# Self-attention of a decoder layer: ends reordered, two repeating loads, and the query product as three fp32r products

## The reference, cut to what matters

```python
def _L0_attn_ref(x, Wq, Wk, Wv, Wu, bu):            # x: (16, 224, 512), 16 heads of 32
    xh = x.reshape(b, t, h, c)
    scale = d ** (-0.25)
    q = jnp.einsum('bthc,oc->btho', xh, Wq) * scale
    k = jnp.einsum('bthc,oc->btho', xh, Wk) * scale
    v = jnp.einsum('bthc,oc->btho', xh, Wv)
    scores = jnp.einsum('bihc,bjhc->bhij', q, k)     # causal mask on j > i
    attn = jax.nn.softmax(scores, axis=-1)
    y = jnp.einsum('bhij,bjhc->bihc', attn, v).reshape(b, t, d)
    return y @ Wu.T + bu

x = _layernorm(x + _L0_attn_ref(x, ...))
x = _layernorm(x + _L0_xattn_ref(x, ctx_1024, ...))  # context of 750 rows
x = _layernorm(x + _L0_ffn_ref(x, ...))              # a gated recurrence over the 16 batches
```

## Time and profile before

| what | value |
| --- | --- |
| profiled execution, own time | 1434.18 us |
| its span | 1432.2 us |
| median of the runs | 1435.0 us |
| PE busy over the span | 1397.3 us (98%) |
| DVE, ACT, POOL busy | 919.4, 731.0, 523.3 us |
| mean granted TensorE clock | 0.994 |

### The profile page before, as it was taken

One profiled execution on the slowest core, in us unless ns is written; L12 is line 12 of the kernel. 1 busy time (PEld: TensorE's weight loads), 2 busy tenths in 40 slices (PEclk: granted clock), 3 DMA queues, 4 the chain that ended last, 5 costly groups with the idle time before them and its releaser, 6 DMA issues.

```text
span 1432.2 us, 28312 instructions
## 1 busy us (share of the span) xinstructions
PE 1397.3 (98%) x9990; PEld 1209.0 (84%) x9990; DVE 919.4 (64%) x1911; ACT 731.0 (51%) x1989; POOL 523.3 (37%) x419
## 2 busy tenths in 40 slices
PE   6999999999989999999999999999999999999997
PEld 3677777777789999999999988999999999999775
DVE  4578888888756776577657762544554445546697
ACT  3478888888646656665666455322222222222232
POOL 2455555555466565565656521000000000010264
PEclk9999999999999999999999999999999999999999
DMA  6123223324466657665766956010110101000353
GB/s 183 34 72 105 78 77 102 84 82 147 133 158 191 202 190 221 204 205 185 227 199 209 211 135 172 1 26 1 26 26 0 26 2 30 30 1 30 95 185 125
DMA packets 133173, 157.92 MB, mean 110 GB/s; under 512 B 62400, under 2 KB 70592, under 8 KB 133104
## 3 DMA queue, kind: packets, MB, share of 16 engines
q1 hardware_dynamic: 133104, 157.01, 37.6%
HBM read 105.61 MB, written 35.78 MB: 99 GB/s over the span
## 4 chain that ended last, share of the span: by engine, by line
PE 90%; issue 3%; POOL 2%; ACT 2%; DVE 2%; SPq 1%; DMA 1%; POOLq 0%; ACTq 0%; DVEq 0%
PE banks L1463 15%; PE banks L1492 10%; PE banks L970 9%; PE banks L954 9%; PE banks L308 7%; PE banks L983 6%; PE banks L940 6%; PE banks L1494 6%; PE banks L279 5%; PE banks L260 3%; PE banks L266 2%; PE banks L291 2%; PE banks L239 2%; PE banks L926 1%; POOL o_r L2038 1%
## 5 line engine op out<-in xcount | busy, mean ns | idle before, releaser
L435 ACT ACTIVATE s_p<-banks,a_nmax 112x224 f32<-112x224 f32 (+1 forms) x512 | 199.1, 414 | 67.2 <-DVE a_nmax L539 64.4
L713 POOL TENSOR_TENSOR s_p<-s_p,a_rinv 112x896 f32<-112x896 f32 (+1 forms) x128 | 164.5, 1306 | 156.9 <-DVE a_rinv L547 151.2
L1580 ACT ACTIVATE f_gate<-f_gate 128x448 f32<-128x448 f32 x90 | 52.2, 580 | 198.6 <-DVE f_gate L1703 198.6
L1437 POOL CAST m_hi<-w_raw 128x2048 fp32r<-128x2048 f32 x1 | 2.3, 2266 | 407.8 <-PE banks L1463 407.8
L1700 DVE TENSOR_TENSOR f_gate<-banks,f_xg_early 128x448 f32<-128x448 f32 x45 | 28.1, 624 | 189.7 <-PE banks L1494 189.7
L1308 POOL TENSOR_TENSOR x_cx_lo<-s_cx_raw,x_cx_hi 125x512 fp32r<-125x512 f32 x96 | 120.7, 1295 | 38.4 <-ACT x_cx_hi L1080 38.4
L538 DVE TENSOR_REDUCE a_nmax<-banks 112x1 f32<-112x224 f32 x256 | 97.7, 381 | 39.3 <-PE banks L266 39.3
L435 ACT ACTIVATION_READ_ACCUMULATOR s_p<-banks,a_nmax 112x1 f32 x512 | 112.9, 220 | 0.0
L279 PE MATMUL banks<-identity,s_p 112*112 112x112 f32 x768 | 104.9, 260 | 0.5 <-ACT a_pt L461 0.5
L279 PEld LDWEIGHTS banks<-identity,s_p 112*112 112x112 f32 x768 | 87.6, 133 | 21.0 <-issue 2.7
L1301 POOL TENSOR_TENSOR s_ct<-s_ct_raw,s_ct 128x750 fp32r<-128x750 f32 x60 | 97.6, 1657 | 0.0
(11 more groups left out here) (243 smaller groups left out, 3638.4 us busy)
## 6 DMA issues: line engine op xcount, KB each, us to landing
s_ct_raw<-in_ct SPq DMA_DIRECT2D x16, 1500.0 KB, 6.7
s_cx_raw<-in_cx SPq DMA_DIRECT2D x16, 1500.0 KB
a_xt<-in_xt SPq DMA_DIRECT2D x16, 448.0 KB, 4.0
a_xrow<-in_x SPq DMA_DIRECT2D x16, 448.0 KB, 3.5
a_xres<-in_x SPq DMA_DIRECT2D x16, 448.0 KB, 4.6
x_scratch<-a_xn SPq DMA_DIRECT2D x16, 448.0 KB, 3.1
x_scratch<-x_xn SPq DMA_DIRECT2D x16, 448.0 KB, 4.7
x_halves<-x_halves SPq DMA_DIRECT2D x16, 448.0 KB, 3.1
```

Source lines behind the costliest of these rows:

```text
L435: e = act.activation((p1 if c else p0)[:, g, h, :], src, ACT.Exp, bias=nmax[:, g % 2, c, h:h + 1], accum_out=rsum[:, g % 2, c, h:h + 1])
L713: pool.tensor_tensor(p[:, g, :, :], p[:, g, :, :], inv, ALU.mult).then_inc(norm_done, 1)
```

## The change

- The Wq and Wk copies are loaded by one DMA each, with a source that repeats.
- PE does not wait for `const_ready` 6 (the identity) before its first product, but after `z(0)`; ACT waits for 2 instead of 6.
- In steps 0 and 1 the second weight job stands behind `t` and `z` instead of ahead of them.
- From `z(5)` on (27 of 32) the query product is three fp32r products. POOL forms the high and low halves of x^T one step ahead (a cast and a subtraction, 128 x 448), after its `normalise`; the halves of A are formed once. POOL waits for the z product before (`z_done`) and for the DMA of x^T ahead of its second multiplication in those steps.
- `separate_ahead` stands behind the opening of the projection; the four context casts of ACT stand one step later, behind the opening of the last batch's projection; `first_z_low` of DVE stands one step earlier.

```diff
+        ZS = 5
+        def in_parts(m):
+            return not isinstance(m, int) or m >= ZS
...
-            for j in range(G):
-                sp.dma_start(wq4[:, j, :], io["wq"]).then_inc(w_in, 16)
-                sp.dma_start(wk4[:, j, :], io["wk"]).then_inc(w_in, 16)
+            for copies, w in ((wq4, "wq"), (wk4, "wk")):
+                sp.dma_start(copies[:], io[w].rearrange("p (a d) -> p a d", a=1).to_broadcast((C, G, C))).then_inc(w_in, 16)
...
-            pe.wait_ge(const_ready, 6)
-            pe.wait_ge(w_in, 2 * G * 16)
+            pe.wait_ge(w_in, 2 * 16)
...
-                mm = pe.matmul(ps_z[:, 0:2 * T], a_diag[:], xt[:, odd, 2 * j:2 * j + 2, :], start=True, stop=True)
+                if in_parts(m):
+                    wait(pe, parts_done, 2 * m + 2)
+                    pe.matmul(ps_z[:, 0:2 * T], a_hi[:], z_hi[:], start=True, stop=False)
+                    pe.matmul(ps_z[:, 0:2 * T], a_lo[:], z_hi[:], start=False, stop=False)
+                    mm = pe.matmul(ps_z[:, 0:2 * T], a_hi[:], z_lo[:], start=False, stop=True)
+                else:
+                    mm = pe.matmul(ps_z[:, 0:2 * T], a_diag[:], xt[:, odd, 2 * j:2 * j + 2, :], start=True, stop=True)
...
-                if n in (0, 1) and slot in (0, 4):
-                    job(WU + 2 * n + slot // 4, 0)
+                if n in (0, 1) and slot in (0, 5):
+                    job(WU + 2 * n + slot // 5, 0)
...
+            def first_context():
                 act.wait_ge(shared.ct_in, 16)
                 act.wait_ge(t_done, 3 * STEPS)
                 for k in range(KC):
...
-                    if isinstance(n, int) and n == STEPS:
-                        separate_ahead()
...
                     if g == 2:
                         open_projection(b - 1, 0)
                         z_copy(2 * b + 2, 0)
+                    if isinstance(n, int) and n == STEPS:
+                        separate_ahead()
+                    if isinstance(n, int) and n == STEPS + 2:
+                        first_context()
...
-                    if isinstance(n, int) and n == 4 * (B + 1) + 3:
+                    if isinstance(n, int) and n == STEPS + 6:
                         first_z_low()
...
+            def query_parts(m, odd, j):
+                pool.tensor_copy(z_hi[:], xt[:, odd, 2 * j:2 * j + 2, :]).then_inc(parts_done, 1)
+                wait(pool, parts_done, 2 * m + 1)
+                pool.tensor_tensor(z_lo[:], xt[:, odd, 2 * j:2 * j + 2, :], z_hi[:], ALU.subtract).then_inc(parts_done, 1)
...
+                    if c == 0 and m is not None:
+                        wait(pool, z_done, m)
+                        wait(pool, xt_in[odd], 16 * landed)
...
+                    split = g % 2 == 1 and in_parts(m) and within(m, PAIRS)
```

More of the change, by code:

```diff
@@ L65, in self_attention @@
         wv_diag = sb("wv_diag", [128, 128])
+        a_hi, a_lo = (sb("a_" + part, [128, 128], F32R) for part in ("hi", "lo"))
+        z_hi, z_lo = shared.z_in
         wu_raw = shared.wu_raw
@@ L102, in self_attention @@
         job_done = sem("job_done")
-        wv_round = sem("wv_round")
+        parts_done = sem("parts_done")
         w_in = sem("w_in")
@@ L378, in tensor @@
             z(0, 0, 0, 1)
+            pe.wait_ge(const_ready, 6)
             def steps(i, odd):
@@ L420, in scalar @@
             act.wait_ge(prep_mm, 1)
-            act.wait_ge(const_ready, 6)
+            act.wait_ge(const_ready, 2)
             for g in range(G):
@@ L702, in early, with normalise @@
                         pool.wait_ge(raw_in[2], 16)
[L703 to L707, removed]
+                    pool.tensor_copy(shared.wv_hi[:, k, :], raw[2][:, k, :]).then_inc(parts_done, 1)
+                    pool.wait_ge(parts_done, 2 * k + 3)
+                    pool.tensor_tensor(shared.wv_lo[:, k, :], raw[2][:, k, :], shared.wv_hi[:, k, :], ALU.subtract).then_inc(parts_done, 1)
+            def query_parts(m, odd, j):
+                pool.tensor_copy(z_hi[:], xt[:, odd, 2 * j:2 * j + 2, :]).then_inc(parts_done, 1)
+                wait(pool, parts_done, 2 * m + 1)
+                pool.tensor_tensor(z_lo[:], xt[:, odd, 2 * j:2 * j + 2, :], z_hi[:], ALU.subtract).then_inc(parts_done, 1)
+            def normalise(n, g, m=None, odd=None, landed=None):
                 if not within(n, STEPS):
@@ L721, in power, with steps @@
                 wait(pool, rstd_done, b + 1)
-            def steps(b):
+            def steps(i, odd):
+                b = 2 * i + odd
                 for g in range(NG):
                     n = NG * b + g
-                    normalise(n - 1, (g - 1) % NG)
+                    m, m_odd, landed = (2 * b + 2, 1 - odd, i + odd + 1) if g == 1 else (2 * b + 3, 1 - odd, i + odd + 1)
+                    split = g % 2 == 1 and in_parts(m) and within(m, PAIRS)
+                    if split:
+                        normalise(n - 1, (g - 1) % NG, m, m_odd, landed)
+                    else:
+                        normalise(n - 1, (g - 1) % NG)
                     if isinstance(n, int):
                         early(n)
+                    if split:
+                        if isinstance(m, int) and m == ZS:
+                            pool.wait_ge(parts_done, 2 * KC + 2)
+                        query_parts(m, m_odd, g // 2)
                     if g == 3:
@@ L741, in first_context_low @@
                 low.then_inc(shared.ctl_done, 1)
[L743 to L749, removed]
+            pool.wait_ge(prep_act, 1)
+            pool.tensor_copy(a_hi[:], a_diag[:]).then_inc(parts_done, 1)
+            pool.wait_ge(parts_done, 1)
+            pool.tensor_tensor(a_lo[:], a_diag[:], a_hi[:], ALU.subtract).then_inc(parts_done, 1)
+            for b in range(4):
+                steps(b // 2, b % 2)
+            with pool.Fori(2, B // 2 - 1) as i:
+                for odd in range(2):
+                    steps(i, odd)
+            for b in range(B - 2, B + 2):
+                steps(b // 2, b % 2)
         return Stage(sync, tensor, scalar, vector, gpsimd)
@@ L2094 @@
     x1t: object
+    z_in: object
     dot: object
@@ L2233, in decoder @@
                 ahead_halves=at("ahead_halves", raw_at[2] - arena_at, [R, TC, 2, D], U16),
+                z_in=tuple(at(f"z_in{i}", raw_at[2] - arena_at + 4 * TC * D + 8 * T * i, [128, 2, T]) for i in range(2)),
                 x1t=at("x1t", raw_at[2] - arena_at + 4 * TC * D, [128, KC, T], F32),
```

## The result

The changed kernel takes 1423.7 us, median of four runs (1421.7 to 1426.0), against 1434.2 of the kernel before beside it: ratio 0.993, 95% interval 0.992 to 0.994. Forecast were 1423.0 and a range of 1419.5 to 1430. Its profiled execution took 1423.75 us with a span of 1421.9; before, 1434.18 and 1432.2. So 10.3 us of span went. A total that comes out right does not show that its terms did, so I cut the span at four instructions of TensorE that both kernels have: the first product of the job with the key bias (29.23 before), the last transposes that close self-attention's first part (374.95), the first scores of cross-attention (397.08) and its first product with the values (417.35).

A forecast was written before the change was run, and what follows sets the result against it. PE was taken to bound steady self-attention, with chains of waits at both ends. Opening 4.5, query product 4.6 less 0.6, and end 3.0 gave 11.5 us off 1434.2, so 1423 us; range 1419.5 to 1430.

The forecast's parts named there:

- The opening: Start of the kernel: fewer DMA issues and reordered weight jobs gain 4.5 us, range 2.5 to 5.5.
- the loads: Opening: six DMA issues less bring SP's later issues, the key bias included, 2.8 us earlier, worth 2.8 us.
- z with the jobs: Opening, steps 0 and 1: z and transposes ahead of the second weight job gain 1.0 and about 1.1 us.
- the low clock: Opening: step 1's scores, moved earlier, may fall in TensorE's 1.2 GHz spell and take about 1 us more.
- The copy of 27.23: Opening, step 1: the copy that ran at 27.23 us would come near 22.7.
- The query product: Self-attention: three fp32r products replace two fp32 passes, saving 0.17 us in each of 27 products, 4.6 us.
- The wait of `norm`: Steps with g = 1: DVE's `norm`, slowed by POOL's subtraction, loses 0.05 us in each of 12 batches, 0.6 us.
- the middle: Steady self-attention: 4.6 us from the query products less 0.6 us for DVE's `norm` gives a gain of 4.0 us.
- The end: End of self-attention: three moved pieces of work bring the first cross-attention scores 3.0 us earlier, range 1.9 to 3.2.
- the three terms: End of self-attention: moving `separate_ahead` gains 0.8 us, the context casts 0.4, `first_z_low` 1.9.
- The thin cover: End of self-attention: POOL's context halves finish half a microsecond before PE needs them; otherwise 0 to 1 us is lost.
- only the ends gain: Rival: the middle gains nothing, through the DVE and ACT loop or the `norm` stall; 7.5 us off, 1427.5, chance 0.17.

The follow-up runs named there:

- loads_only: The kernel before the change with only the eight small weight loads replaced by two repeating loads; 1432.5 us, one run.
- after_again: The changed kernel run again without any edit, on another chip; 1425.1 us, ratio 0.995.
- norm_moved: The changed kernel with the second `norm` of each batch moved from the step with g = 1 to g = 2; 1423.1 us, ratio 0.992.
- parts_unused: The changed kernel with POOL still forming the halves but PE running the fp32 query product without them; 1426.0 us, ratio 0.994.
- products_only: The kernel before the change with only the 27 query products split into three fp32r parts, opening and end as before; 1434.4 us, ratio 0.999.
- ends_only: The changed kernel with all 32 query products in fp32 and no halves on POOL, opening and end as changed; 1425.8 us, ratio 0.993.
- end_ahead_back: The changed kernel with `separate_ahead` put back ahead of the opening of the projection; 1430.2 us, one run.

## Why the prediction was right, and which step of it failed

**The opening, 4.5 forecast, 4.73 measured.** Right in size in this profile; over the nine it is 3.0 to 5.6, about the range that I gave (2.5 to 5.5). Its parts were not what I wrote: the loads are worth 1.16 us alone and z with the jobs 3.03, against 2.8 and 2.1. I had put the low clock down as 1 us that the scores may meet. They met it with the loads alone, and in three of the nine. The key bias landed later than forecast in the changed kernel, DVE's spread starting at 11.78 and not at 10.7 (10.56 in loads_only, 11.19 in after_again): it was issued at 5.68, 2.78 us earlier as worked out, but was 6.0 us under way instead of 5.0. The copy of 27.23 runs at 21.72, 1 us earlier than foreseen.

**The query product, 4.6 forecast.** The size of the product was right within 0.02 to 0.04 us: in norm_moved a step with one takes 5.34 and 5.35 us instead of 5.48 and 5.49, so about 0.14 and not 0.17. The first fp32r product behind the transposes is followed after 0.28 to 0.31 us, not the 0.203 that I took for all three from the recurrence. Three of these: 0.30 + 0.20 + 0.30 = 0.80 us from the first start to the scores'. But the other steps did not stay as they were, as I had said they would: 4.97 and 4.98 became 5.01 and 5.02. Net a product brings 0.10 us even in norm_moved, by estimate 2.8 us for 27 of them and not 4.6. I had read 0.56 us of idle DVE as "PE is late, not DVE", with a slack in every step. The loop's slack was 0.15 us, and only in every second step; the x7 of the earlier trace rows was already its fourth head waiting for ACT.

**The wait of `norm`, 0.6 forecast, all of it measured.** This is the step that failed: "ACT has a gap there and the scores need the exponentials only at the end of the step, so I take 0.05 us lost in each of 12 batches". The length was as forecast (0.8 to 1.4 us; 1.37 to 1.50 measured), the idle time ahead of the maxima was gone as forecast. But the end of the step is where the last exponential was needed: it was closed at 296.89, after the next scores had started. I had looked for a gap of ACT and not for the distance between the last exponential and the fourth head's score, which the trace before has: 0.15 us. Loss 0.21 us a batch (2.28 in eleven), not 0.05, and with it the whole gain: the middle's 4.0 us came to nothing from the products. The Trainium skill (SBUF — State Buffer, "Who interferes with whom") names the exclusion of the two engines and gives the ports to whichever comes first, for its whole instruction. The rows agree that the two collide. They do not agree on who goes first: `norm` starts first, at 290.27, and is stretched all the same, while the subtraction takes the 1.15 us that it also takes in norm_moved, away from `norm`. In the eleven batches of the changed kernel and of parts_unused `norm` starts between 0.07 us ahead of the subtraction and 0.18 behind it, and ends 0.28 us after it each time.

**The end, 3.0 forecast, 3.05 measured.** Each of the three terms was within 0.1 us. The thin cover held: the first scores wait 0.37 us, for DVE's `s_first`, not for POOL's context halves.

**The sum.** Without the products the forecast would have been 7.5 us, the rival "only the ends gain", 1427.5. What carried the result to 1423.7 is 1.7 us in 40 to 70 us, from a shorter spell at half clock, and 0.7 behind the first cross-attention scores, where such spells differ from run to run. No term of mine stands for them. The first comes with the changed opening as far as the traces go: all the profiles that have slots or loads as changed but one show 0.94, the kernel before and products_only 0.89. That makes the total of the forecast right by 2.4 us that it did not foresee, in place of 4.0 that it did; that is luck. ends_only, which is that rival, was measured at 1425.8, 9.3 us below its own median before and not 7.5; by ratio (0.993) it cannot be told from the changed kernel.

What stays open: why the one spell is sometimes 6.8 us long and sometimes 3.4. end_ahead_back had the long one with the same opening.

## What to carry to other kernels

Before a product is made cheaper by giving another engine more work, look at what the other engines do beside that work, and measure from the last result of the loop to the instruction that needs it: a wait that costs nothing today may stand exactly where tomorrow's gain should be. And look at the records of the step itself: here the scores that fell apart into x7 and x1 were an engine that already waited.

When an engine's idle time is filled at the start, its clock may stay up: of the 3.03 us of a moved job, 0.93 were the job's own. It need not: three of nine equal openings had the half clock all the same. A part of a few us that one profile shows is then compared over several.

And a total that agrees is checked by stretches: two errors, here −4.0 and +2.4 us, can stand in a sum of 11.5 that is 1.2 off.

## What the runs showed of the hardware that I had not expected

- POOL's subtraction of 1.15 us stretched a DVE instruction of 0.54 us that had begun 0.07 us earlier to 1.50 us; with the start a little otherwise (parts_unused) to 1.37. Whichever of the two began first, the DVE instruction ended 0.28 us after the subtraction, in 22 of 22 cases.
- Spells at half clock last 3.4 or 6.8 us in the stretch from 40 to 70 us, with PE busy for 29.6 us or more of 30; the same code has different ones in its two profiles (19.57 and 21.61 us to the first product with the values), which is more than most edits here are worth.
- The 2 KB load of the key bias was 6.0 us under way in the changed kernel and 5.0 before; the other kernels with two repeating loads ahead of it have 4.8 to 6.3, so fewer pieces ahead did not set it.
- The three fp32r products of 128 x 448 took 0.80 us in the middle of fp32 work, where 24 of them in a row took 0.20 each: the first start to the second was 0.28 to 0.31 us, and the third to the next scores 0.30.
